# A transformer layer on one core: another order of work in the turn, and x1 turned by VectorE and a DRAM scratch

## The reference, cut to what matters

```python
# x: (16, 512, 256), 32 heads of 8
qkv = relu(x @ qkv_weight.T)                  # q, k, v
v_pad = concat([v, 1])
vk   = einsum('bnhe,bnhd->bhed', v_pad, k)    # linear attention, no softmax
vk_q = einsum('bhed,bnhd->bnhe', vk, q)
att  = vk_q[..., :8] / (vk_q[..., 8:] + 1e-15)
x1   = layernorm(x + att @ proj_weight.T + proj_bias)
wg, wu, wd = w_gate / 127, w_up / 127, w_down / 127
h    = silu(x1 @ wg.T) * (x1 @ wu.T)          # 768 hidden
out  = layernorm(x1 + h @ wd.T)
```

## Time and profile before

| | |
|---|---|
| median of three runs | 548.8 us (547.83 to 551.16) |
| the profiled execution | 549.34 us |
| its span, first to last instruction | 547.5 us |
| granted TensorE clock, mean | 0.998 of full speed |
| TensorE matmuls busy | 97% of the span |
| VectorE busy | 72% |
| ScalarE busy | 40% |
| POOL busy | 15% |
| DMA moved | 29.04 MB, 53 GB/s |

### The profile page before, as it was taken

The page is one execution under the profiler, slowest core; times in us unless marked ns, Lnnn a source line. Parts: engine busy times, 40 slices in busy tenths (PEclk is TensorE's granted clock), DMA queues, the critical chain, the costliest instruction groups (busy, mean ns, idle before and its releaser), DMA issues.

```text
span 547.5 us, 9297 instructions
## 1 busy us (share of the span) xinstructions
PE 533.1 (97%) x3531; PEld 465.8 (85%) x3531; DVE 392.7 (72%) x885; ACT 221.4 (40%) x376; POOL 80.4 (15%) x94
## 2 busy tenths in 40 slices
PE   8889999999999999999999999999999999999995
PEld 4777989898898988989898898988989898898975
DVE  5777858587684957858587684957858587684976
ACT  3365243442525435243542524435243542524431
POOL 2001110011100111110011100111110011100212
PEclk9999999999999999999999999999999999999999
DMA  8400120202112030121202112030121202102011
GB/s 296 166 0 3 40 78 29 87 0 77 38 38 77 0 112 3 38 77 31 84 0 77 38 38 77 0 110 5 38 77 37 78 0 77 38 0 79 1 40 40
DMA packets 8653, 29.04 MB, mean 53 GB/s; under 512 B 960, under 2 KB 1728, under 8 KB 8640
## 3 DMA queue, kind: packets, MB, share of 16 engines
q1 hardware_dynamic: 8640, 28.85, 14.8%
HBM read 20.46 MB, written 8.39 MB: 53 GB/s over the span
## 4 chain that ended last, share of the span: by engine, by line
PE 93%; DVE 4%; ACT 1%; issue 1%; DMA 1%; POOL 0%; POOLq 0%; SPq 0%
PE abcd_ps L585 45%; PE gate_ps L585 17%; PE up_ps L585 16%; PE abcd_ps L625 6%; PE abcd_ps L633 5%; PE abcd_ps L614 3%; DMA wq_raw<-w_q 1%; DVE x1T_lo L337 0%; PE abcd_ps L732 0%; DVE h L344 0%; ACT silu L241 0%; DVE st L567 0%; DVE st L400 0%; DVE r L563 0%; DVE att L377 0%
## 5 line engine op out<-in xcount | busy, mean ns | idle before, releaser
L344 DVE SCALAR_TENSOR_TENSOR h<-up_ps,silu 128x512 f32<-128x512 f32 x96 | 66.1, 688 | 79.1 <-ACT silu L241 79.1
L241 ACT ACTIVATE silu<-gate_ps 128x512 f32<-128x512 f32 x96 | 57.4, 597 | 98.3 <-PE gate_ps L585 98.3
L585 PE MATMUL abcd_ps<-wd_hi,h_hi 128*128 128x256 f32 x384 | 93.1, 283 | 0.8 <-DVE h_lo L337 0.8
L585 PE MATMUL abcd_ps<-wd_hi,h_lo 128*128 128x256 f32 x384 | 92.9, 283 | 0.0
L585 PE MATMUL gate_ps<-x1T_hi,wg_hi 128*128 128x512 f32 x192 | 79.4, 414 | 2.0 <-DVE x1T_lo L337 1.9
L337 DVE TENSOR_TENSOR h_lo<-h,h_hi 128x512 fp32r<-128x512 f32 x96 | 66.1, 689 | 14.4 <-ACT h_hi L236 11.2
L585 PE MATMUL up_ps<-x1T_hi,wu_hi 128*128 128x512 f32 x192 | 75.1, 391 | 0.0
L585 PE MATMUL up_ps<-x1T_lo,wu_hi 128*128 128x512 f32 x192 | 75.0, 391 | 0.0
L585 PE MATMUL gate_ps<-x1T_lo,wg_hi 128*128 128x512 f32 x192 | 74.9, 390 | 0.0
L585 PEld LDWEIGHTS abcd_ps<-wd_hi,h_hi 128*128 128x128 f32 x384 | 73.7, 192 | 1.1 <-DVE h_lo L337 1.0
L585 PEld LDWEIGHTS abcd_ps<-wd_hi,h_lo 128*128 128x128 f32 x384 | 73.7, 192 | 0.0
(11 more groups left out here) (119 smaller groups left out, 945.2 us busy)
## 6 DMA issues: line engine op xcount, KB each, us to landing
x_raw<-x_tok SPq DMA_DIRECT2D x16, 512.0 KB, 3.2
xT_raw<-x_chan SPq DMA_DIRECT2D x15, 512.0 KB, 3.3
out<-out_sb SPq DMA_DIRECT2D x15, 512.0 KB, 2.6
wg_raw<-w_gate SPq DMA_DIRECT2D x1, 768.0 KB, 6.3
wu_raw<-w_up SPq DMA_DIRECT2D x1, 768.0 KB, 7.8
wd_raw<-w_down SPq DMA_DIRECT2D x1, 768.0 KB, 9.1
xT_raw<-x_chan SPq DMA_DIRECT2D x2, 256.0 KB, 3.6
wkv_raw<-w_kv SPq DMA_DIRECT2D x1, 512.0 KB, 5.5
```

Source lines behind the costliest of these rows:

```text
L241: nc.scalar.activation(silu[:, j % 2, :], gate_ps[j % 2][:], ACT.Silu, scale=WSCALE).then_inc(silu_ok[j], 1)
L344: nc.vector.scalar_tensor_tensor(out=h[:, j, :], in0=up_ps[j % 2][:], scalar=WSCALE, in1=silu[:, j % 2, :], op0=ALU.mult, op1=ALU.mult).th ...
L585: last = mm(dst, lhsT, rhs, start=start and n == 0, stop=stop and n == len(pairs) - 1)
```

## The change

It has these parts.

1. TensorE's turn gets another order. `ffn_half(i)`: gate_up blocks 0 to 3, att transposes, blocks 4 and 5, projection. `attention_half(i)`: q of batch i+1 (now in A and B), kv tiles 0 to 3 (CC, D, A, B), down tiles 0 and 1 of batch i-1, `vk_of(i+1)`, down tiles 2 and 3, `num_of(i+1)`. Down now writes `gate_ps[1]` and `up_ps[1]` (`down_ps`), so gate_up block 1 waits for both `r2_ok`; the up half of a block waits for `h_ok`, the gate half only for `silu_ok`.
2. x1 of the batches 1 to 14 is not transposed by TensorE any more. VectorE normalizes r1 in place (`x1_of(i, r1)`), then turns it in 32x32 blocks with one instruction into `x1_sq` (`x1_blocks`). SP writes this to a scratch `x1_way` in DRAM with four DMAs, one for each 32 partitions (128 KB each, in runs of 512 bytes), waits for them, and reads it back with one DMA of 512 KB into `x1T_raw`. ScalarE rounds from there (`x1T_hi_spread`), VectorE subtracts from there (`x1T_lo_spread`), both reading runs of 32 elements. A further DMA copies r1 into x1 after r2 of the batch before is made, for the next turn's `r2_add`; `r1_of` waits for it. `x1_sq` and `x1T_raw` lie over the raw weights, which are no longer used then. Batch 15, and batch 0, still go over TensorE.
3. VectorE's and SP's queues are reordered to match; the store of out and the loads go ahead of the new DMAs, and the wait for the store moves from SP to VectorE's `out_of`.
4. Semaphores of single tiles in the last batch are merged into one each.

The core of the diff:

```diff
+        x1_sq = in_place_of(wu_raw).rearrange("p (c n) -> p c n", c=NCB)
+        x1T_raw = in_place_of(wd_raw).rearrange("p (k n) -> p k n", k=KC)
+        x1_way = nc.dram_tensor("x1_way", (P, KC, NG, P), FP32, kind="Internal").ap()
+        down_ps = (gate_ps[1][:], up_ps[1][:])
...
+        def x1T_spread(k):
+            return x1T_raw[:, k, :].rearrange("p (g t s) -> p t g s", g=NG, t=NT)
+        def by_token(T, k):
+            return T[:, k, :].rearrange("p (t g s) -> p t g s", g=NG, t=NT)
...   SP
+            def spread_x1(b):
+                sp.wait_ge(x1_sq_ok, b)
+                for g in range(NG):
+                    sp.dma_start(x1_way[:, :, g, :].rearrange("(j c) k n -> c k j n", j=NG),
+                                 x1_sq[g * SQ:(g + 1) * SQ].rearrange("c (k j) n -> c k j n", k=KC)).then_inc(x1_away, 16)
+                sp.wait_ge(x1_away, 16 * NG * b)
+                sp.dma_start(x1T_raw, x1_way.rearrange("p k g n -> p k (g n)")).then_inc(x1T_in, 16)
+            def turn(i):
+                any_i = not isinstance(i, int)
+                if any_i or i >= 2:
+                    sp.wait_ge(out_ok, i - 1)
+                    sp.dma_start(out[i - 2], out_sb[:].rearrange("p t c -> p (t c)")).then_inc(stored, 16)
+                if any_i or i + 1 < NB:
+                    sp.wait_ge(xb_ok, i + 1)
+                    sp.dma_start(x_raw[:], x[i + 1]).then_inc(x_in, 16)
+                if any_i or i + 2 < NB:
+                    load_xT(i + 2)
+                if any_i or 0 < i < NB - 1:
+                    spread_x1(i)
+                    sp.wait_ge(r2_ok[1], i)
+                    sp.dma_start(x1[:], r1[:]).then_inc(x1_copied, 16)
...   ScalarE
-                    kv_relu(0, i + 1, A)
-                    kv_relu(1, i + 1, B)
-                x1T_hi_of(i)
-                if qkv:
-                    kv_relu(2, i + 1, A)
-                    kv_relu(3, i + 1, B)
+                    for t, bank in enumerate((CC, D, A, B)):
+                        kv_relu(t, i + 1, bank)
+                    x1T_hi_spread(i)      # waits for up_mm[NH - 1] and x1T_in
...   VectorE
+            def x1_blocks(b):
+                dve.wait_ge(x1_ok, b + 1)
+                nc.vector.transpose(x1_sq.rearrange("p c (t s) -> p t c s", t=NT),
+                                    r1[:].rearrange("p t (c s) -> p t c s", s=SQ)).then_inc(x1_sq_ok, 1)
+            def x1T_lo_spread(b):
+                for k in range(KC):
+                    dve.wait_ge(x1T_hi_ok[k], b + 1)
+                    minus_hi(by_token(x1T_lo, k), x1T_spread(k), by_token(x1T_hi, k)).then_inc(x1T_lo_ok[k], 1)
+            def ffn_half(i):
+                att_of(i)
+                h_of(i - 1, 0)
+                if not isinstance(i, int) or i > 1:
+                    out_of(i - 2)
+                h_of(i - 1, 1)
+                h_lo_of(i - 1, 0, 1)
+                h_of(i - 1, 2)
+                if not isinstance(i, int) or i < NB - 1:
+                    xT_lo_of(i + 1)
+                h_of(i - 1, 3)
+                attT_lo_of(i)
                 h_lo_of(i - 1, 2, 3)
                 h_of(i - 1, 4, 5)
+            def attention_half(i):
+                r1_of(i)
+                dve.wait_ge(st1_ok, i + 1)
+                nc.vector.tensor_copy(st1_seen[:], st1[:, NT - 1, 0:1])
+                aggregated(st1, mv1, mv1_ok)
                 h_lo_of(i - 1, 4, 5)
+                x1_of(i, r1)
+                x1_blocks(i)
                 r2_add(i - 1, 0, x1)
                 dve.wait_ge(r2_ok[0], i)
                 stats(st2, r2, 0)
+                vk_of(i + 1)
                 r2_add(i - 1, 1, x1)
                 dve.wait_ge(r2_ok[1], i)
                 stats(st2, r2, 1, st2_ok)
                 dve.wait_ge(st2_ok, i)
+                x1T_lo_spread(i)
                 aggregated(st2, mv2, mv2_ok)
...   TensorE
+                    if j == 1 and (not isinstance(b, int) or b > 0):
+                        pe.wait_ge(r2_ok[0], b)
+                        pe.wait_ge(r2_ok[1], b)
...
+            def ffn_half(i):
+                gate_up(i - 1, 0, 1, 2, 3)
+                attT_of(i)
+                gate_up(i - 1, 4, 5)
+                proj_of(i)
+            def attention_half(i):
+                pe.wait_ge(xT_lo_ok, i + 2)
+                q_of(i + 1)
+                for t, bank in enumerate((CC, D, A, B)):
+                    if t < 2:
+                        pe.wait_ge(r1_ok[t], i + 1)
+                    else:
+                        pe.wait_ge(q_ok[t - 2], i + 2)
+                    kv_of(t, i + 1, bank)
+                down_of(i - 1, (0, 1))
+                vk_of(i + 1)
+                down_of(i - 1, (2, 3))
+                num_of(i + 1)
```

More of the change, by code:

```diff
@@ L23 @@
 NH = HID // P
+SQ = 32
+NG, NCB = P // SQ, C // SQ
 BANK = 512
@@ L173, in _ @@
             sp.dma_start(wd_raw[:], down_w).then_inc(wd_in, 16)
[L174 to L178, removed]
+            turn(0)
+            turn(1)
+            with sp.Fori(2, NB - 2) as i:
+                turn(i)
+            turn(NB - 2)
+            turn(NB - 1)
+            turn(NB)
             for t in range(NT):
-                sp.wait_ge(out_tile[t], 1)
+                sp.wait_ge(out_tile, t + 1)
                 sp.dma_start(out[NB - 1][:, t * C:(t + 1) * C], out_last[:, t, :]).then_inc(stored, 16)
@@ L409, in r1_of @@
             def r1_of(b, pairs=False):
+                if not isinstance(b, int) or b > 1:
+                    dve.wait_ge(x1_copied, 16 * (b - 1))
                 dve.wait_ge(xb_ok, b + 1)
@@ L427, in r2_add @@
                 nc.vector.scalar_tensor_tensor(
-                    out=pair(r2, n), in0=(A, B)[n], scalar=WSCALE, in1=pair(x1_of_b, n), op0=ALU.mult, op1=ALU.add).then_inc(r2_ok[n], 1)
+                    out=pair(r2, n), in0=down_ps[n], scalar=WSCALE, in1=pair(x1_of_b, n), op0=ALU.mult, op1=ALU.add).then_inc(r2_ok[n], 1)
             def normed(dst, r, mv, rs, ok, tiles=range(NT)):
@@ L440, in out_of @@
             def out_of(b):
+                if not isinstance(b, int) or b > 0:
+                    dve.wait_ge(stored, 16 * b)
                 dve.wait_ge(rstd2_ok, b + 1)
@@ L504, in second_part @@
                 dve.wait_ge(st2_ok, i)
-                x1_of(i, x1)
+                x1T_lo_spread(i)
                 aggregated(st2, mv2, mv2_ok)
[L507 to L524, removed]
-            i = NB - 1
[L528 to L537, removed]
+            for i in (1, 2):
+                ffn_half(i)
+                attention_half(i)
+            with dve.Fori(3, NB - 1) as i:
+                ffn_half(i)
+                attention_half(i)
+            i = NB - 1
+            ffn_half(i)
             h_lo_of(i - 1, 4, 5)
@@ L667, in gate_up @@
                     add_up(gate, gate_hi[:-1], stop=False)
+                    if j >= 2:
+                        pe.wait_ge(h_ok[j - 2], b + 1)
                     add_up(up, up_hi[:-1], stop=False)
@@ L689, in down_of @@
             def down_of(b, tiles=range(NT)):
+                pe.wait_ge(h_ok[NH - 1], b + 1)
                 for t in tiles:
-                    last = down_part(b, t, range(NH), (A, B)[t // 2][:, (t % 2) * C:(t % 2 + 1) * C])
+                    last = down_part(b, t, range(NH), down_ps[t // 2][:, (t % 2) * C:(t % 2 + 1) * C])
                     if t % 2:
                         last.then_inc(down_mm[t // 2], 1)
-            def last_part(i):
-                down_of(i - 1)
-                pe.wait_ge(xT_lo_ok, i + 2)
-                q_of(i + 1, free=r1_ok)
-                for t in range(2):
-                    pe.wait_ge(r2_ok[t], i)
-                    kv_of(t, i + 1, (A, B)[t])
-                pe.wait_ge(q_ok[KC - 1], i + 2)
-                x1T_of(i, x1)
-                for t in range(2, NT):
-                    pe.wait_ge(kv_ok[t - 2], i + 2)
-                    kv_of(t, i + 1, (A, B)[t % 2])
-            def first_part(i):
-                gate_up(i - 1, 0)
-                vk_of(i)
-                gate_up(i - 1, 1)
-                num_of(i)
-            def middle_part(i):
-                gate_up(i - 1, 2, 3)
+            def ffn_half(i):
+                gate_up(i - 1, 0, 1, 2, 3)
                 attT_of(i)
@@ L793, in _ @@
                     for t in (2 * n, 2 * n + 1):
-                        last = nc.tensor.transpose((CC, D)[k][:, t * P:(t + 1) * P],
+                        last = nc.tensor.transpose((A, B)[k][:, t * P:(t + 1) * P],
                                                    x1_last[:, t, k * P:(k + 1) * P], ident)
@@ L800, in _ @@
             gate_up(i, *range(NH))
-            pe.wait_ge(r2_ok[1], i)
             for t in range(2):
```

94 lines of the change are left out of this document (41 added, 53 removed).

## The result

| | before | after |
|---|---|---|
| median | 549.16 us (7 runs) | 553.22 us (7 runs, 552.43 to 555.23) |
| ratio | | 1.008, 95% interval 1.006 to 1.010 |
| profiled execution, span | 549.34, 547.5 | 555.23, 553.3 |
| granted TensorE clock | 0.998 | 0.995 |

The time rises by 0.8%; 553.4 was forecast. The page of the changed kernel: TensorE's busy time falls while the span grows.

The account below looks back on a forecast made before the run. The prediction took TensorE's stream to bound the kernel, its matmuls busy 97% of the span. 549.3 - 12.2 for removed transposes + 16.8 for stalls gave 553.9, as median 553.4 us; range 551.5 to 562.

Parts of the forecast that it names:

- The removed work: Eight x1 transposes a batch leave TensorE in batches 1 to 14: 0.87 us a turn, 12.2 us gained.
- The seam: From down's last matmul to gate_up, VectorE needs 3.19 us, TensorE 1.99: a stall of 1.20 us a turn, 16.8 in all.
- The projection: Its wait for attT_lo: ready over 0.3 us before TensorE comes, so no cost, or 0 to 3 us if a wait was missed.
- the turn without waits: TensorE's turn with the transposes gone and the other groups costing what they had: 32.82 - 0.87 = 31.95 us.
- The way through DRAM: x1's block transpose, four writes and read, up to x1T_hi: hidden with 2.7 us to spare, so no cost.
- The rule on strided transposes: For the scratch writes: judged not to bite; by it a write would take an estimated 32 us, a turn about 60.
- The sum: 549.3 - 12.2 + 16.8 = 553.9 us profiled, 553.4 as median, 0.84% more.
- (d): Rival: no stall before gate_up, x1T_lo being ready when num ends, so 536.6 us; chance 0.03.
- (e): Rival: no change, the stall before gate_up just equals the 0.87 us removed, so 548.8 us; chance 0.03.
- (b): Rival: the DRAM path comes last before gate_up, 559 or 609 us by how the writes land; chance 0.13.
- (c): Rival: other waits within the turn, attT_lo or vk_of, cost 0.3 to 0.6 us a turn, 558 to 562 us; chance 0.09.

Follow-up runs that it names:

- pe_turn: The changed kernel without block transpose, DRAM writes and read; TensorE transposes x1 again between down's tiles 2 and 3 and num: 554.59 us, ratio 1.0098.
- light_pe: light without block transpose and DRAM scratch; TensorE transposes x1 between down's tiles 2 and 3 and num: 547.14 us, ratio 0.9979.
- light: lo_first with r2's bn_stats and bn_aggr moved into VectorE's wait before attT_lo and out_of moved behind the block transpose: 543.42 us, ratio 0.9897.
- lo_first: The changed kernel with both x1T_lo on VectorE put ahead of the last two bn_stats, behind r2_add(1): 553.39 us, ratio 1.0074.
- light_late: light with the store of out issued after the copy of r1 into x1, not straight behind the scratch read: 540.24 us, ratio 0.9849.
- no_way: The changed kernel without the four DRAM writes and the read, x1T made from block-transposed x1 in SBUF (output wrong): 552.97 us, ratio 1.0093.
- read_twice: The changed kernel with the scratch read issued again once the first has landed, ScalarE waiting for both: 597.55 us, ratio 1.088.

## Why the prediction was right

**The removed work.** 0.87 us a turn was read off the steps, and pe_turn and light_pe show it as 0.88 (271.16 to 272.04) and 0.87 (267.11 to 267.98).

**The seam.** This term carried the forecast, 1.20 us a turn, and it measured 1.20. Its parts, forecast and seen: r2_add 0.32 and 0.31, stats 0.72 and 0.73, the step behind them 0.79 and 0.78, two x1T_lo 1.30 and 1.29, the release 0.06 and 0.06; TensorE's side 1.99 and 1.97. The choice to price the strided SBUF source by the plain rows was right, the runs of 32 cost nothing. The turn came out at 33.17 against 33.15. That it is so near is partly luck, as the next paragraph shows.

**The projection.** Over 0.3 us of room was forecast, and it was gone. attT_lo starts at 285.75 and ends at 287.04; gate_up's last matmul starts at 286.85 and at its step of 0.23 is done at 287.08; the projection starts at 287.10. The two sides arrive within some hundredths of a us of each other. The failing step is out_of's 1.30: it took a step of 1.64 (278.52 to 280.16), because POOL's xb (276.72 to 279.12) now runs beside it. Before, xb ran beside att, and att kept its length. The overlap is short (0.60 us here), but out_of's length follows it: 1.34 us without any in light, 1.56 with 0.44 in lo_first, 1.73 with 0.60 here.

What it cost can be read at the projection. It starts 0.02 us late, and its first matmul, whose weights had to wait (0.3 us at the longest), takes a step of 0.22 us (253.93 to 254.15) where light_late and light_pe, without this wait, show 0.12: 0.12 to 0.13 us a turn, 1.8 us in all, inside the 0 to 3 us that the prediction left open. The sum had nothing for it. It came out even so because a second term was off the other way: the turn without waits is not 31.95 us but 33.17 - 1.20 - 0.13 = 31.84, and light_late says the same with 32.13 - 0.28 = 31.85. The forecast let the reordered groups cost what they had cost, and the new order is cheaper by about a tenth: light_pe, with all the transposes and no stall, has a turn of 32.74 where the kernel before has 32.82. The two errors cancel. With this room gone, lo_first gave its gain back in full.

**The way through DRAM.** Hidden, as forecast, but with 1.1 us to spare instead of 2.7. From the projection's first matmul (253.93): mv1 came at 5.6 (5.3 forecast), rstd1 at 7.6 (6.7), x1 at 9.05 (8.1), x1_sq_ok at 10.3 (9.3), the read's issue at 14.9 (13.0), x1T_hi's start at 18.1 (16.3); it was wanted at 19.9 less its own 0.64. Two terms were mis-sized (0.3 us more is in mv1). POOL's pair of instructions took 0.55 and 1.34 us, where the second took 1.02, with VectorE's h_lo running beside it (0.9 us of waiting on x1). And four issues took 2.58 us, 0.65 each, where a store took 0.36, with 2.6 to landing. The block transpose, which had no row, took 1.25 us against 1.2 assumed. The rule on strided transposes of the Trainium skill ("VectorE: DVE Perf Modes", section "The three transpose paths") warns of copies with a large innermost destination stride. It did not bite here: with runs of 512 bytes the four writes and the read take 7.7 us together (264.29 to 272.02). No run here has a DMA with such a stride, so none tests the rule itself. The forecast's estimate by it also set the factor of 19 on a plain store's 1.7 us, while the Trainium skill gives it, in that section, against the crossbar transpose of the DMA.

**The sum.** 553.4 forecast, 553.22 measured. That they agree to 0.2 us is luck: two terms of 0.1 us a turn cancel, the median of the kernel before was 548.8 us in the forecast's three runs and 549.16 in seven, and the seven runs of the changed kernel have a spread of 2.8 us. The stall of 1.20 us a turn, which decides the sign, is the mechanism's own. As for the rivals, (d) and (e) are excluded by the seam's rows, (b) by no_way, and (c) contributed 0.13 us a turn, not 0.3 to 0.6.

## What to carry to other kernels

Work taken off the bound engine is a gain only if the wait at the next handover is shorter than what was taken; so price the handover as a race between the two queues from their last common event, with all that stands ahead of the awaited instruction in program order. An instruction that nobody waits for (a statistic, an output, a store) costs its full length when it stands there. When it is moved, check where the queue next has no room: here the first try won 0.92 us and gave back 0.85, and only moving the work into idle time, and the store away from the read, made it 13 us. Then ask again what comes last: once VectorE's queue was mended, the path through DRAM was next, a few tenths of a us behind it.

## What the runs showed of the hardware that was not expected

- VectorE's and POOL's instructions on SBUF data are longer where they overlap: four normalizations of 128x256 from SBUF to SBUF take 1.73 us with 0.60 us of POOL's xb beside them (changed kernel), 1.56 with 0.44 (lo_first) and 1.34 without (light). POOL's ve and rstd take 0.55 and 1.34 us beside h_lo, whose two sources are in SBUF, but 0.20 and 1.02 beside attT_lo (light, 276.91), which reads PSUM. Only out_of was moved to test it; for POOL's pair the rows are all there is.
- A granted clock of half speed, for some 3 to 4 us, after a single idle gap of TensorE in read_twice: after the seven gaps of 3.13 to 5.14 us, and after two of the seven of 2.57 to 2.83 us. With gaps of 0.94 us in every turn it was not seen in the turns of the changed kernel. It also follows the idle times ahead of batch 0's gate_up in some executions and not in others: light_late, pe_turn and no_way then need 13.5 us from there to the projection, the rest 11.9 to 12.0.
- A read of 512 KB from DRAM with a store of 512 KB issued 0.6 us behind it: 3.8 to 4.2 us from its issue to the next instruction that uses it (13 turns of light), against 3.1 to 3.2 without the store (14 turns of light_late).
- An issue of a four-dimensional DMA of 256 runs took SP 0.65 us; one of 512 KB in plain rows took 0.34 between DRAM and SBUF and 0.52 from SBUF to SBUF.
